# The first stage of a conditioned feed-forward kernel streams the columns of its matmuls in another order

## The reference

```python
h = gelu(einsum('btel,elf->btef', x.reshape(B, T, 8, 128), W1) + b1)   # 128 -> 512 in each group
y = einsum('btef,efl->btel', h, W2) + b2                               # 512 -> 128 in each group
scale, shift = split(silu(emb) @ emb_W + emb_b)
hn = layernorm(y.reshape(B, T, 1024), ln_g, ln_b) * (1 + scale) + shift
out = x + silu(hn) @ out_W + out_b                                     # 1024 -> 1024
```

## Time and profile before

| | |
|---|---|
| median of 2 runs | 719.15 us (719.0 to 719.31) |
| the profiled execution's own time | 720.29 us |
| its span, first to last instruction | 718.1 us |
| TensorE busy | 712.6 us, 99% of the span |
| ACT busy | 452.4 us, 63% |
| DVE busy | 526.2 us, 73% |
| granted TensorE clock, mean | 1.000 |

### The profile page before, as it was taken

One profiled execution on the slowest core, in us unless ns is written; L12 is line 12 of the kernel. 1 busy time (PEld: TensorE's weight loads), 2 busy tenths in 40 slices (PEclk: granted clock), 3 DMA queues, 4 the chain that ended last, 5 costly groups with the idle time before them and its releaser, 6 DMA issues.

```text
span 718.1 us, 8148 instructions
## 1 busy us (share of the span) xinstructions
PE 712.6 (99%) x3144; PEld 580.6 (81%) x3144; DVE 526.2 (73%) x553; ACT 452.4 (63%) x494; POOL 103.0 (14%) x70
## 2 busy tenths in 40 slices
PE   8999999999999999999999999999999999999998
PEld 6888878888788887788878888888888888888886
DVE  6887887888757789889876687666866578668721
ACT  6777867778677787897973465434654356446610
POOL 0000000000000011110012323322132222323300
PEclk9999999999999999999999999999999999999999
DMA  5277444863413723133179566765556745665641
GB/s 178 86 265 230 140 159 152 281 216 114 147 59 118 240 82 118 59 117 108 39 270 286 162 202 165 205 215 199 154 165 205 223 170 142 199 204 151 192 127 59
DMA packets 47078, 118.55 MB, mean 165 GB/s; under 512 B 3648, under 2 KB 24128, under 8 KB 43968
## 3 DMA queue, kind: packets, MB, share of 16 engines
q1 hardware_dynamic: 41760, 100.73, 39.9%
q0 software_dynamic: 4608, 16.78, 11.9%
q10 hardware_dynamic: 672, 0.52, 0.3%
HBM read 67.69 MB, written 33.55 MB: 141 GB/s over the span
## 4 chain that ended last, share of the span: by engine, by line
PE 92%; DVE 3%; ACT 3%; issue 1%; DMA 1%; ACTq 0%
PE psum L809 47%; PE psum L724 21%; PE psum L740 21%; PE psum L821 2%; DVE g_lo L527 1%; ACT g_hi L383 1%; ACT g_raw L377 1%; PE psum L751 1%; DVE g_hi L525 1%; DVE xT_lo L515 1%; ACT xT_hi L369 1%; DMA wraw<-in_W 1%; PE psum L776 0%; DVE sq L557 0%; DVE yb L566 0%
## 5 line engine op out<-in xcount | busy, mean ns | idle before, releaser
L527 DVE TENSOR_TENSOR g_lo<-g_raw,g_hi 128x1024 fp32r<-128x1024 f32 x128 | 156.7, 1225 | 64.2 <-ACT g_hi L383 61.8
L377 ACT ACTIVATE g_raw<-psum,cols 128x1024 f32<-128x1024 f32 x128 | 142.8, 1116 | 63.7 <-PE psum L724 48.7
L809 PE MATMUL psum<-oW_lo,s_hi 128*128 128x512 f32 x496 | 152.8, 389 | 0.0
L809 PE MATMUL psum<-oW_hi,s_lo 128*128 128x512 f32 x496 | 152.7, 389 | 0.0
L809 PE MATMUL psum<-oW_hi,s_hi 128*128 128x512 f32 x496 | 152.7, 389 | 0.0
L740 PE MATMUL psum<-g_hi,W 128*128 128x512 f32 x512 | 137.3, 390 | 0.0
L724 PE MATMUL psum<-xT_hi,W 128*128 128x512 f32 x508 | 137.0, 392 | 0.1
L724 PEld LDWEIGHTS psum<-xT_hi,W 128*128 128x128 f32 x508 | 95.6, 189 | 22.1 <-issue 2.2
L740 PEld LDWEIGHTS psum<-g_hi,W 128*128 128x128 f32 x512 | 95.9, 188 | 20.9 <-DVE g_hi L525 0.8
L809 PEld LDWEIGHTS psum<-oW_lo,s_hi 128*128 128x128 f32 x496 | 93.1, 188 | 19.4
L809 PEld LDWEIGHTS psum<-oW_hi,s_lo 128*128 128x128 f32 x496 | 93.1, 188 | 19.4
(11 more groups left out here) (70 smaller groups left out, 638.1 us busy)
## 6 DMA issues: line engine op xcount, KB each, us to landing
y_scratch<-y_stage SPq DMA_DIRECT2D x32, 512.0 KB, 3.0
yb<-y_scratch SPq DMA_DIRECT2D x16, 1024.0 KB, 4.8
res<-in_x SPq DMA_DIRECT2D x32, 512.0 KB, 5.7
res<-out_b_all POOLq DMA_DIRECT2D x32, 512.0 KB, 4.9
xT_raw<-in_xT SPq DMA_DIRECT2D x31, 512.0 KB, 4.4
out<-res SPq DMA_DIRECT2D x31, 512.0 KB, 2.9
emb_raw<-in_emb_W SPq DMA_DIRECT2D x8, 1024.0 KB, 7.3
wraw<-in_out_W SPq DMA_DIRECT2D x16, 256.0 KB, 4.8
```

The source lines that it names most:

```text
L377: nc.scalar.activation(g_raw[:, m % 2], ring(m), ACT.Gelu, bias=cols[:, R_B1 + k:R_B1 + k + 1]).then_inc(gelu_done, 1)
L527: nc.vector.tensor_tensor(g_lo[:, m % 2], g_raw[:, m % 2], g_hi[:, m % 2].bitcast(F32), ALU.subtract).then_inc(glo_done, 1)
L809: mm = nc.tensor.matmul(proj(q)[:, half], v[:, g, cut], w[:, g, half], start=(g == 0 and k == 0), stop=(g == G - 1 and k == 2))
```

## The change

For group g a pair (run, skip) is listed. Of each half of 512 columns, the moving operand of `first` and `second` is read in runs of `run` neighbouring columns that lie `run * skip` columns apart; then the next such set. With skip 1 (group 0) the order stays. `taken` is this view of an SBUF tile. The results stand in PSUM in the order in which they were streamed, one after another. `gelu` and `stage_y` read PSUM as it stands and write `g_raw` and `y_stage` through `taken`, so that the tiles in SBUF are in natural order again; `left` gives the PSUM operand the same three-dimensional shape. Both become two ACTIVATEs of 512 columns, in group 0 too, and only the second one sets the semaphore. Weights, rounding, the DMAs, the second stage and the first six matmuls (line 776) stay.

```diff
+        RUN_SKIP = [(16, 1), (16, 16), (16, 2), (16, 8), (1, 256), (32, 8), (8, 32), (64, 4)]
+        def taken(ap, g):
+            run, skip = RUN_SKIP[g]
+            if skip == 1:
+                return ap
+            return ap.rearrange("p (o i r) -> p i o r", i=skip, r=run)
+        def left(ap, g):
+            run, skip = RUN_SKIP[g]
+            if skip == 1:
+                return ap
+            return ap.rearrange("p (i o r) -> p i o r", i=skip, r=run)
...
-                nc.scalar.activation(g_raw[:, m % 2], ring(m), ACT.Gelu,
-                                     bias=cols[:, R_B1 + k:R_B1 + k + 1]).then_inc(gelu_done, 1)
+                g = ORDER[n][0]
+                for h in range(2):
+                    half = slice(h * BANK, (h + 1) * BANK)
+                    done = nc.scalar.activation(taken(g_raw[:, m % 2, half], g), left(ring(m)[:, half], g), ACT.Gelu,
+                                                bias=cols[:, R_B1 + k:R_B1 + k + 1])
+                done.then_inc(gelu_done, 1)
...
-                nc.scalar.activation(y_stage[:, n % 2], y_psum(n), ACT.Identity,
-                                     bias=cols[:, R_B2 + g:R_B2 + g + 1]).then_inc(y_staged, 1)
+                for h in range(2):
+                    half = slice(h * BANK, (h + 1) * BANK)
+                    done = nc.scalar.activation(taken(y_stage[:, n % 2, half], g), left(y_psum(n)[:, half], g),
+                                                ACT.Identity, bias=cols[:, R_B2 + g:R_B2 + g + 1])
+                done.then_inc(y_staged, 1)
...
-                        mm = nc.tensor.matmul(ring(m)[:, half], W[:, g % WS, w, cut], v[:, n % 2, half],
+                        mm = nc.tensor.matmul(ring(m)[:, half], W[:, g % WS, w, cut], taken(v[:, n % 2, half], g),
                                               start=(k == 0), stop=(k == 2))
...
-                        mm = nc.tensor.matmul(y_psum(n)[:, half], W[:, g % WS, w, cut], v[:, m % 2, half],
+                        mm = nc.tensor.matmul(y_psum(n)[:, half], W[:, g % WS, w, cut], taken(v[:, m % 2, half], g),
                                               start=(c == 0 and k == 0), stop=(c == C - 1 and k == 2))
```

## The result

735.29 us (734.6 to 735.97, 2 runs) against 719.15: slower by 16.1 us, ratio 1.0223 [1.0206, 1.0239]. The sign was right; the time was forecast at 761.6. The profiled execution took 735.97 us, its span 733.8.

What follows compares the result with a forecast made beforehand. TensorE was taken to bound the kernel: 41.0 us for group 4's single columns plus 1.5 us for ACT, on the median of 719.15, gave 761.6 us. The range was 718 to 769, the likeliest case's own 758 to 768.

Steps and rivals of the forecast that it cites:

- That TensorE sets the end: Whole kernel: TensorE's matmul pitch of 226.7 ns sets the time; ACT's slowdown is paid only past its slack.
- I take half pace for single columns: Group 4's 192 matmuls, reading single columns, take 213.3 ns more each: 41.0 us, bounds 0 and 95.
- The row for half pace: Profile row for six matmuls at the start, 2.72 us or 453 ns each, taken as the trace's half pace.
- Runs of eight and more: nothing: TensorE reads in groups 1 to 3 and 5 to 7: 0 us, since at most one read in eight is a step.
- The third rival: Every break between runs costs TensorE, one column time each: 59 us, 780 us in all; dearer cases' chance 0.15.
- The 1.5 us: First stage, late, where ACT also begins the layernorm: doubled ACTIVATEs make TensorE late by 1.5 us, bounds 0 and 5.
- I take 0: ACT's stepped writes of group 4's columns, 1024 bytes apart: 0, bounds 0 and 0.43 us per half.
- The rule on lines of 16 bytes: SBUF reads need two hits per 16-byte line for full bandwidth: group 4 loses, groups 1 to 3 and 5 to 7 don't.
- The first rival: TensorE reads group 4's single columns at full pace, only ACT's cost is left: 721 us, 719 to 729; chance 0.25.

Runs made afterwards that it cites:

- e2: Changed kernel's orders at TensorE, but gelu and staging of y as the one contiguous ACTIVATE of the kernel before: 728.03 us, ratio 1.0128.
- e4: Kernel before with operands altered by group (half the columns, fewer or stepped weights, columns in steps of 2, 16, 128): 452, 434, 283 ns for those column steps.
- e8: Kernel before, groups 1 to 7 alternating two single-column streams 2 to 128 columns apart: 216 ns a matmul from distance 4 to 128, 227 at 2.
- e10: Groups 0, 1: two streams 256 apart advancing by 2, 4 columns; groups 2, 3: columns repeated; ACT's write orders varied. Pitches 227, 452, 216, 216 ns.
- e1: Changed kernel with natural order in all groups, the two ACTIVATEs kept: 722.05 us against 718.97, ratio 1.0042.
- e3: All groups in the order 0, 256, 1, 257, with one ACTIVATE each that puts the columns back in SBUF: 790.3 us, ratio 1.0993.
- e6: Kernel before, first stage alone streaming 0, 256, 1, 257, with x transposed laid out ahead so ACT works as before: 710.56 us, ratio 0.9869.
- e7: Kernel before, both stages streaming 0, 256, 1, 257, with x transposed and out_W laid out ahead, ACT and DVE as before: 706.11 us, ratio 0.9817.
- e13: Kernel before, first stage streaming 0, 4, 1, 5 in blocks of 8; ACT reads PSUM in steps of two, writes SBUF in order: 707.11 us, ratio 0.9837.
- e12: Kernel before with columns doubled in broken runs, or weights cut or stepped, by group: 216 ns in groups 0 to 2, 236 with weights in steps of four.

## Why the prediction was wrong

**That TensorE sets the end** held: the changed pitch went into the time (9.3 us by the table, 9.1 in e2). The sign came out right by luck: the term of 41.0 us that gave it measured -2.0, and the 16.1 us came from terms that were put at 0 or 1.5.

**"I take half pace for single columns", 41.0 us: the step that failed.** It measured -2.0 us. The price was carried from line 544 on DVE by the argument that a reader that barely keeps 1.04 ns a column can't keep 0.417. But the row said nothing of which columns TensorE fetches together. e4 shows that half pace exists (434 and 452 ns); e8 and e10 show that it depends on how many columns of a 16-byte line every second column finds, and group 4 happens to be the best case.

**The row for half pace was misread.** The earlier trace rows gave 453 ns as a mean over 2.72 us. The starts in the trace are 427 ns apart in five cases of six, with one gap of 591, and 427 ns is 512 columns at 1.2 GHz, the lower level of the clock, not a slow reading. The clock column shows 1.00 there, but the trace's records of the granted clock begin only at 9.81 us, and there the distance falls from 426 ns to 234. In the changed kernel, e1 and e2 the 427 ns end within one matmul of the first record too (10.10, 7.37 and 6.86 us); in e3, e4, e6, e7 and e13, whose records begin at 4.3 to 5.6 us, before the first of the six matmuls, no two starts among them are more than 338 ns apart. So the row gave no price for a stepped read. That 427 ns has no 13 ns on top fits a fetch that has time to spare at that pace, though no run tests it.

**"Runs of eight and more: nothing"** measured 11.3 us (the table without group 4). The third rival had the mechanism, breaks between runs, with 16 us for these groups (59 less 43.5). e12 bounds it: breaks cost only where each fetch finds two columns of a line, not four. Why 32 breaks cost 13 ns in group 1 and 5 in group 3, and natural order 11 ns with none, stays open.

**ACT.** A half takes the 685 ns that were worked out. The pairs alone, forecast at 22 to 40 us of ACT time, added 21.2 in e1 (473.6 - 452.4), just under the lower end; the changed kernel added 37.5 (489.9 - 452.4), since a pair of group 4 takes 2.11 us against 1.26, and its 20 pairs (16 of gelu, 4 of y) come to 20 x 0.85 = 17 us on top. The 1.5 us that it was to make TensorE late are 3.1 by themselves (e1), inside the bounds of 0 and 5, but spread over items 22 to 31 and not mostly in the stretch named. The stepped writes, "I take 0", measured just past the upper bound: 0.51 us a half against the 0.43 given. They cost 5.3 us. The forecast hid them behind 10.2 us by which TensorE was to be slower in each item of group 4, and it was not slower there; that this alone would have hidden them no run shows.

**The rule on lines of 16 bytes.** In group 4 every column lies in another line than the one before, and it gained 10.4 ns a matmul; groups 1, 2, 3, 5 and 6 fill whole lines, and they lost 4.7 to 16.4. The Trainium skill (SBUF — State Buffer, "Door 1: The DMA port swizzle") asks for two hits in a line of 16 bytes. The 16 bytes are what e8 and e10 measure, but counted over every second column of the stream, and four are better than two; the measurement decides. The Trainium skill gives N / 2.4 + 2.5 ns as the gap of an isolated matmul (TensorE: Matmul & The Clock Gate, "Back-to-back issue gap"), an estimate of 215.8 for 512 columns: the orders at 216 agree with it, and natural order at 226.7 does not.

**The first rival** (single columns at full pace, 721) was right for TensorE in group 4 and gave up to 8 us for ACT's writes, which cost 5.3; with 11.3 us for the runs it lacked it would have been near.

## What to carry to other kernels

Read the pitch of matmuls against columns / clock before believing that a busy TensorE is at its best: here pieces of six matmuls, 1.36 us each and without a gap between them, hid 11 ns in every matmul, and an order of reading that gives every second column a full 16-byte line took it back (e13, 1.6%). When an engine must undo an order, let it step through PSUM (steps of two columns were free here) and write SBUF in order. And what a faster stage frees has to be looked for in the next one: in e7 the second stage's matmuls became faster and the stage took as long as before, because the layernorm's chain, 1.6 us slower per pass than the new matmuls, had only its lead to hide behind.

## What the hardware showed unexpectedly

- One fp32r operand, one size, one clock column of 1.00, and from 216 to 452 ns a matmul by the order of its columns alone; natural order (226.7) is not the fastest.
- With weights read in steps of 16 bytes a matmul took 236 ns under both orders (e4, e12); with 64 or 32 columns of weights it took 229 and 232 in natural order, more than with 128.
- ACT writing lone columns to SBUF: 1145 to 1206 ns for 512 columns, against 682 in order; reading PSUM in steps of two columns: 1113 ns for 1024, as in order (1116).
